# A gated delta-rule layer: two fp32 column sums on TensorE become pairs of rounded-and-rest matmuls, ScalarE and GpSimd queues are reordered, and the gates are computed another way

## Reference, cut to what matters

```
xn   = layernorm(x)
q, k, v = silu(conv4(xn @ Wq)), silu(conv4(xn @ Wk)), silu(conv4(xn @ Wv))
q, k = q / sqrt(sum(q*q) + 1e-6) * 128**-0.5,  k / sqrt(sum(k*k) + 1e-6)
g    = -exp(A_log) * softplus(xn @ Wf1 @ Wf2 + dt_bias)      # 8 decay groups a head
beta = sigmoid(xn @ Wb)
for t: S = S*exp(g);  delta = beta*(v - k.S);  S += k (x) delta;  o = q.S
y    = o * silu(xn @ Wg + bg)
y    = y * rsqrt(mean(y*y) + 1e-5) * norm_w
x1   = x + y @ Wo
out  = x1 + MoE(layernorm(x1))     # 2 of 6 experts per batch row
```

## Time and profile before

| | |
|---|---|
| median of 3 runs | 5799.16 us (5796.24 to 5802.64) |
| the profiled execution's own time | 5794.63 us |
| its span, first to last instruction | 5792.9 us |
| busy share of the span: PE, DVE, ACT, POOL | 96%, 77%, 52%, 30% |
| granted TensorE clock, mean | 0.987 of full speed |
| gates block | to 222.9 us |
| units | 222.9 to about 4976 us |
| mixture | from there to the end |

### The profile page before, as it was taken

One profiled execution on the slowest core, in us unless ns is written; L12 is line 12 of the kernel. 1 busy time (PEld: TensorE's weight loads), 2 busy tenths in 40 slices (PEclk: granted clock), 3 DMA queues, 4 the chain that ended last, 5 costly groups with the idle time before them and its releaser, 6 DMA issues. The chain is left out here.

```text
span 5792.9 us, 89715 instructions
## 1 busy us (share of the span) xinstructions
PE 5546.4 (96%) x30136; PEld 3878.3 (67%) x30136; DVE 4480.6 (77%) x9483; ACT 3000.7 (52%) x5573; POOL 1735.1 (30%) x1766
## 2 busy tenths in 40 slices
PE   5599999999999999999999999999999999899999
PEld 2377777777777777777777777777777777444444
DVE  7688888888888888888888888888888888211110
ACT  3456666665556566666666666555656665201110
POOL 2233333333333333333333333333333333000000
PEclk8799999999999999999999999999999999999999
DMA  2101110101111111111111111111111110231221
GB/s 76 46 28 37 30 37 28 36 27 36 30 37 30 37 30 36 31 30 37 30 37 30 36 29 35 28 37 30 37 30 38 30 30 24 99 111 51 78 76 49
DMA packets 183711, 235.84 MB, mean 41 GB/s; under 512 B 25048, under 2 KB 128088, under 8 KB 179168
## 3 DMA queue, kind: packets, MB, share of 16 engines
q1 hardware_dynamic: 111072, 188.22, 10.8%
q10 hardware_dynamic: 72192, 41.95, 2.4%
HBM read 183.75 MB, written 46.38 MB: 40 GB/s over the span
## 5 line engine op out<-in xcount | busy, mean ns | idle before, releaser
L685 PE MATMUL bank<-xT,weights 128*128 128x512 f32 x4096 | 2125.4, 606 | 33.5 <-PEq L155 33.5
L1339 POOL TENSOR_TENSOR KR<-KR,decay_u 128x256 f32<-128x256 f32 x768 | 632.2, 823 | 1544.3 <-PE bank L712 1534.5
L712 PEld LDWEIGHTS bank<-KQ,KR 128*128 128x128 f32 x7168 | 906.3, 191 | 191.5 <-issue 180.9
L712 PE MATMUL bank<-KQ,KR 128*128 128x128 f32 x7168 | 960.7, 276 | 7.0 <-DVE KQ L965 6.1
L950 DVE SCALAR_TENSOR_TENSOR conv<-pre,taps,conv 128x512 f32<-128x512 f32 x1152 | 935.8, 812 | 17.2 <-ACT conv L1167 8.0
L965 DVE TENSOR_TENSOR KQ<-KQ,decay_u 128x512 f32<-128x512 f32 x896 | 788.9, 880 | 143.9 <-PE bank L712 143.0
L987 DVE COPY_PREDICATED all_pairs<-level_mask,bank 128x256 f32<-128x256 int32 x1792 | 822.6, 523 | 0.0
L685 PEld LDWEIGHTS bank<-xT,weights 128*128 128x128 f32 x4096 | 662.8, 191 | 186.3 <-issue 164.0
L736 PEld LDWEIGHTS bank<-T_inv,pairs 128*128 128x128 f32 x1536 | 270.4, 189 | 535.8 <-ACT T_inv L1213 290.4
L736 PE MATMUL bank<-T_inv,pairs 128*128 128x128 f32 x1536 | 495.4, 407 | 82.5 <-ACT T_inv L1213 81.9
L1213 ACT ACTIVATE T_inv<-bank 128x256 fp32r<-128x256 f32 x640 | 247.2, 386 | 601.7 <-PE bank L754 597.6
(11 more groups left out here) (168 smaller groups left out, 9214.4 us busy)
## 6 DMA issues: line engine op xcount, KB each, us to landing
decay_u<-decay_scratch SPq DMA_DIRECT2D x128, 510.0 KB
beta_u<-beta_scratch SPq DMA_DIRECT2D x128, 256.0 KB
y_scratch<-y_rn ACTq DMA_DIRECT2D x128, 256.0 KB, 2.3
y_in<-y_scratch SPq DMA_DIRECT2D x32, 1024.0 KB, 4.8
xt<-in_L_attn_hidden_states SPq DMA_DIRECT2D x8, 1024.0 KB, 5.3
x_in<-in_L_attn_hidden_states SPq DMA_DIRECT2D x32, 256.0 KB, 5.1
out<-o_out ACTq DMA_DIRECT2D x32, 256.0 KB, 2.0
w<-in_L_ffn_W SPq DMA_DIRECT2D x8, 704.0 KB, 5.0
```

The source lines that it names most:

```text
L685: last = nc.tensor.matmul(bank[w % 2][:], weights[par][:, w, k, :], xT[:, k, u % J * UC:(u % J + 1) * UC], start=k == 0, stop=k == KC - 1)
L712: last = nc.tensor.matmul(to[:, :, i], KR[:, cols(i)], second if i < COUPLES else second[:, :, ::-1, ::-1], start=True, stop=True)
L1339: nc.gpsimd.tensor_tensor(firsts, firsts, second.to_broadcast([P, 2, UC >> (l + 2), 1 << l]), ALU.mult).then_inc(keys_scaled.sem, 1)
```

## The change

- `diagonal` no longer multiplies tiles. GpSimd forms the elementwise product of KR and q_hat (`diagonal_product`), ScalarE rounds it to fp32r (`round_diagonal`, now first in its step), GpSimd takes the exact rest (`diagonal_left`), and PE sums both over partitions with a tile of ones. It moves behind `level(2)`, as does `keep_diagonal` on DVE (before `scale(2)`).
- `y_sums` is done in the same way, with `y_squares_left` on GpSimd; the 1/128 moves into the logarithm.
- ScalarE's order: `take_t(4)` and `take_x(4)` come before `square_output` and `silu_gate`; the key square comes behind `take_t(5)`.
- GpSimd's order: `squares_left` of queries and keys moves from before levels 5 and 6 to behind levels 3 and 4; the one of y stands behind level 5.
- Gates: beta is computed as 64 rows of 128 (batch row by head) instead of 16 rows of 512, log(1+e) by a polynomial of degree 11 without a reciprocal, the two stores have a semaphore each, Wf1's product comes before beta's on PE, and ScalarE computes the next chunk's inverse deviation before it touches the decay logits.

```diff
+
+
+        LOG1P = [1.0, -0.4999997913837433, 0.33332496881484985, -0.24986496567726135,
+                 0.19885820150375366, -0.16087622940540314, 0.12377995997667313, -0.08188040554523468,
+                 0.04100657254457474, -0.013187825679779053, 0.001986696384847164]
+        SP_STEPS = len(LOG1P)
 
...
                 sp.wait_ge(beta_steps, j * 2 + 2)
-                sp.dma_start(beta_scratch[:, bass.ds(j, 1), :].rearrange("h a c -> h (a c)"),
-                             b_out[:]).then_inc(scratch_stored, 16)
...
-                dve.wait_ge(scratch_stored, j * 32 + 32)
+                dve.wait_ge(beta_stored, j * 16 + 16)
                 nc.vector.reciprocal(b_out[:], b_den[:]).then_inc(beta_steps, 1)
...
                 dve.wait_ge(z_exp_ready, j + 1)
-                chained(1, nc.vector.tensor_scalar(z_s[:], z_exp[:], 2.0, None, ALU.add))
-                chained(2, nc.vector.reciprocal(z_s[:], z_s[:]))
-                chained(3, nc.vector.tensor_tensor(z_s[:], z_s[:], z_exp[:], ALU.mult))
-                chained(4, nc.vector.tensor_tensor(z_s2[:], z_s[:], z_s[:], ALU.mult))
-                chained(5, nc.vector.tensor_scalar(z_sum[:], z_s2[:], ATANH[-1], None, ALU.mult))
-                for k, c in enumerate(ATANH[-2:0:-1]):
-                    chained(6 + k, nc.vector.scalar_tensor_tensor(z_sum[:], z_sum[:], c, z_s2[:], ALU.add, ALU.mult))
-                chained(SP_STEPS, nc.vector.scalar_tensor_tensor(z_sum[:], z_sum[:], ATANH[0], z_s[:], ALU.add, ALU.mult))
+                chained(1, nc.vector.tensor_scalar(z_sum[:], z_exp[:], LOG1P[-1], None, ALU.mult))
+                for k, c in enumerate(LOG1P[-2::-1]):
+                    chained(2 + k, nc.vector.scalar_tensor_tensor(z_sum[:], z_sum[:], c, z_exp[:], ALU.add, ALU.mult))
                 nc.vector.scalar_tensor_tensor(softplus[:], z[:], 0.0, z_sum[:], ALU.max,
                                                ALU.add).then_inc(softplus_ready, 1)
...
 
-            def chunk(j, first):
+            def chunk(j, first, last):
                 for k in range(KC):
...
+                act.wait_ge(f1_done, j + 1)
+                nc.scalar.activation(f1_sb[:], bank[4][:], ACT.Copy).then_inc(f1_ready, 1)
                 act.wait_ge(beta_logits_done, j + 1)
                 if not first:
                     act.wait_ge(beta_steps, j * 2 - 1)
-                nc.scalar.activation(b_exp[:], bank[5][0:H, :], ACT.Exp, scale=-1.0).then_inc(beta_exp_ready, 1)
-                act.wait_ge(f1_done, j + 1)
-                nc.scalar.activation(f1_sb[:], bank[4][:], ACT.Copy).then_inc(f1_ready, 1)
+                nc.scalar.activation(b_exp[:], bank[5][0:B * H, 0:P], ACT.Exp, scale=-1.0).then_inc(beta_exp_ready, 1)
                 if not first:
                     decays(j - 1)
+                if not last:
+                    inverse_std(j + 1)
...
-                        last = nc.tensor.matmul(bank[5][0:H, :], wb[:, k, :], xT[:, k, bass.ds(j * UC, UC)],
-                                                start=k == 0, stop=k == KC - 1)
-                    last.then_inc(beta_logits_done, 1)
-                    for k in range(KC):
                         last = nc.tensor.matmul(bank[4][:], wf1[:, k, :], xT[:, k, bass.ds(j * UC, UC)],
                                                 start=k == 0, stop=k == KC - 1)
                     last.then_inc(f1_done, 1)
+                    for k in range(KC):
+                        for b in range(B):
+                            last = nc.tensor.matmul(bank[5][0:B * H, 0:P], wb_each[:, k, b, :],
+                                                    xT[:, k, bass.ds(j * UC + b * P, P)],
+                                                    start=k == 0 and b == 0, stop=k == KC - 1 and b == B - 1)
+                    last.then_inc(beta_logits_done, 1)
                     pe.wait_ge(f1_ready, j + 1)
                     nc.tensor.matmul(bank[6][:], wf2[:], f1_sb[:], start=True, stop=True).then_inc(f2_done, 1)
...
         def load_unit(h, j, odd):
-            sp.dma_start(beta_u[:], beta_scratch[bass.ds(h, 1), bass.ds(j, 1), :].rearrange("a b c -> (a b) c")
-                         .to_broadcast([P, UC])).then_inc(unit_loaded.sem, 16)
+            sp.dma_start(by_batch(beta_u[:]), beta_scratch[j, :, h, :].unsqueeze(0).to_broadcast([P, B, P])) \
...
                     return
-                wait(pe, unit_ready, m, 1)
-                if b is not None:
-                    wait(pe, k_rows_ready, b, 1)
-                for i in range(B):
-                    last = nc.tensor.matmul(bank[4][:, cols(i)], KR[:, cols(i)], in_order(q_hat[:, cols(i)], i), start=True, stop=True)
-                last.then_inc(diag_done.sem, 1)
+                wait(pe, diag_rest_ready, m, 1)
+                wait(pe, pairs_ready, m, 2)
+                nc.tensor.matmul(bank[4][:], ones_r[:], diag_round[:], start=True, stop=False)
+                nc.tensor.matmul(bank[4][:], ones_r[:], diag_rest[:], start=False, stop=True).then_inc(diag_done.sem, 1)
...
-                    wait(pe, pairs_ready, m, l)
+                if l == 1 and b is not None:
+                    wait(pe, k_rows_ready, b, 1)
+                if l >= 2:
+                    wait(pe, pairs_ready, m, l - 1)
+                if l == 3:
+                    wait(pe, diag_kept, m, 1)
                 to = bank[3 + l % 2][:].rearrange("p (k b m s) -> p k b m s", k=2, b=B, s=1 << l)
...
                     wait(pe, sums_taken, a, 2)
-                wait(pe, y_sq_ready, c, 1)
-                nc.tensor.matmul(bank[2][:], mean_ones[:], y_sq[:], start=True, stop=True).then_inc(y_sums_done.sem, 1)
+                wait(pe, y_rest_ready, c, 1)
+                nc.tensor.matmul(bank[2][:], ones_r[:], y_sq[:], start=True, stop=False)
...
             inverse_z(1)
             project(2, (2,))
-            diagonal()
             level(0)
...
             level(2)
+            diagonal()
             inverse_xt(3)
             output()
...
-                if b is not None:
-                    wait_apart(dve, pairs_kept.sem, pairs_kept.at(b, 1), dve_waits_passed)
+                wait_apart(dve, pairs_ready.sem, pairs_ready.at(m, 2), dve_waits_passed)
                 nc.vector.copy_predicated(by_batch(all_pairs[:, 1]), on_each_batch(ident[:].bitcast(I32)),
-                                          by_batch(bank[4][:])).then_inc(pairs_ready.sem, 1)
+                                          by_batch(bank[4][:])).then_inc(diag_kept.sem, 1)
 
...
+                if l >= 1:
+                    wait_apart(dve, pairs_ready.sem, pairs_ready.at(m, l), dve_waits_passed)
+                elif b is not None:
+                    wait_apart(dve, pairs_kept.sem, pairs_kept.at(b, 1), dve_waits_passed)
+                if l == 2:
+                    wait_apart(dve, diag_kept.sem, diag_kept.at(m, 1), dve_waits_passed)
                 for turned in range(2):
...
             correct_delta(0)
             add_identity_to_z(1)
-            keep_diagonal()
...
             correct_delta(1)
             convolve(0, (2,))
+            keep_diagonal()
...
 
-            def silu_squares(w):
+            def silu_keys_queries(w):
                 if a is None:
                     return
                 wait(act, qk_conv_steps, a, (w + 1) * (TAPS - 1))
                 if w == 0 and m is not None:
-                    wait(act, diag_done, m, 1)
+                    wait(act, diag_product_ready, m, 1)
                     wait(act, unit_ready, m, 1)
                 nc.scalar.activation(silu[:, w], conv[:, w].rearrange("p b t -> p (b t)"),
                                      ACT.Silu).then_inc(silu_ready.sem, 1)
+
+            def square(w):
+                if a is None:
+                    return
                 wait(act, silu_ready, a, w + 1)
                 nc.scalar.activation(squares[:, w], silu[:, w], ACT.Square).then_inc(squares_ready.sem, 1)
+
+            def round_diagonal():
+                if m is None:
+                    return
+                wait(act, diag_product_ready, m, 1)
+                if b is not None:
+                    wait(act, diag_done, b, 1)
+                nc.scalar.activation(diag_round[:], diag_product[:], ACT.Copy).then_inc(diag_rounded.sem, 1)
 
             def silu_v():
...
                 wait(act, y_sums_done, c, 1)
-                nc.scalar.activation(y_rn[:], bank[2][:], ACT.Ln, bias=ln_eps[:, 0:1]).then_inc(y_sums_free, 1)
+                nc.scalar.activation(y_rn[:], bank[2][:], ACT.Ln, bias=ln_eps[:, 0:1], scale=1.0 / P).then_inc(y_sums_free, 1)
...
+            round_diagonal()
             silu_v()
             take_t(1)
             take_x(1)
@@ -1291,13 +1333,15 @@
             take_x(2)
             take_t(3)
             take_x(3)
-            silu_squares(0)
+            silu_keys_queries(0)
+            square(0)
+            take_t(4)
+            take_x(4)
             square_output()
             silu_gate()
```

(80 more changed lines are left out.)

37 lines of the change are left out of this document (23 added, 14 removed).

## The result

The changed kernel takes 5813.53 us (median of 9 runs, 5808.74 to 5833.07) against 5799.71 for the kernel before beside it (9 runs, 5796.24 to 5803.55): 1.0031 times as long, 95% interval 1.002 to 1.0041. The prediction said 5725.

A forecast was written before the change was run, and what follows sets the result against it. PE was taken to bound the units, DVE close behind: 5794.6 us less 60 for the gates and 13 for the units made 5721.6; with the median's 4.5 above it 5726, stated as 5725, range 5590 to 5785.

The forecast's parts named there:

- What bounds: Units bound by PE (98% busy) with DVE (89%) close behind; the gates block by something else.
- B: Step from the key taps' end through silu, square and `take_t(5)` to `inverse_z(6)`: 1.65 us, falling to 1.0.
- PE's savings: Diagonal and `y_sums` as fp32r pairs of 0.55 us save PE 0.34 + 0.31 = 0.65 us a step.
- A: Step from level 0's start to the last key tap's end on DVE: 18.16 us, rising to 19.91 through GpSimd collisions.
- C: Rest of the step, from `inverse_z(6)` to the next level 0, PE's stream: 16.90 us, falling to 15.70.
- The gates: Gates block before the units: period 23.3 us falling to 15.2, 60 us saved, between 45 and 66.
- Rival 2: Slower units: GpSimd wins every race; product also holds off a tap and first `scale`, step 37.6, 5854 us; chance 0.10.

The follow-up runs named there:

- no_y_late_keys: `no_y` with GpSimd's square and rest of the keys moved from behind level 4 to behind level 5: 5807.6 us, 1.0009 of the kernel before.
- y_new_old_squares: Changed kernel with GpSimd's query and key squares back before levels 5 and 6, y's pair behind level 3: 5810.09 us, 1.0015 of before.
- fill: Changed kernel plus two fp32 matmuls of zeros per step in PE's wait before `inverse_z(6)`: 5797.38 us, 0.9992 of the kernel before.
- fill_y_new: `y_new_old_squares` plus the same two matmuls of zeros per step in PE's wait: 5744.45 us, 0.9903 of the kernel before.
- no_y: Changed kernel with the sum of y squared in fp32 as before, query and key squares behind levels 3 and 4: 5839.31 us, 1.0066 of before.
- split_y: Changed kernel, query and key squares back before levels 5 and 6, y's product behind level 3, its rest behind level 6: 5619.41 us, 0.9686 of before.
- gates_only: Kernel before plus only the gates part (beta by rows, polynomial logarithm, two semaphores, beta's loads in four pieces): 5746.06 us, 0.991 of before.
- act_order: `gates_only` plus ScalarE's new order alone; diagonal, y sums and GpSimd's order as before: 5670.14 us, 0.9775 of the kernel before.
- no_y_old_squares: Changed kernel with y's sum in fp32 as before and GpSimd's query and key squares before levels 5 and 6: 5643.67 us, 0.9731 of before.

## Why the prediction was wrong

**What bounds.** Right. Stretch B and the 0.17 us that PE waits once the taps are free show the loop named: taps, silu, `take_t(5)`, `inverse_z(6)`.

**PE's savings.** Right: pairs of 0.55 us, and 0.30 of the usual step for y.

**A.** Right: from 2509.19 to the taps' end at 2529.15, 19.96 us (predicted 19.91). The diagonal's rest at L1092 (1.18), the first tap freed (0.80), the wait for the diagonal (0.54; predicted 0.4), `scale(2)` at 0.68 and the two taps at 2.71 all stand as written.

**B.** Right: 2530.13 - 2529.15 = 0.98 us (predicted 1.0).

**C, the step that failed.** Predicted 15.70, measured 37.28 - 19.96 - 0.98 = 16.34. C was taken as PE's stream alone, the C of before less what PE saves. The walk followed POOL's queries' pair into A, but placed the keys' pair, which the change moves to behind level 4, nowhere, and did not ask whether DVE's chain behind the taps (state, halo copy, `scale(4)`, pairs, identity) still comes in time for `inverse_xt(5)`. A usual step of the changed kernel:

```profile
2567.29 0.96 DVE L961 COPY pre<-pre 128x24 f32<-128x24 f32 x1
2568.17 0.68 DVE L989 TENSOR_TENSOR KQ<-KQ,decay_u 128x512 f32<-128x512 f32 x1
```

```profile
2567.18 1.04 POOL L1391 TENSOR_TENSOR conv<-silu 128x512 f32<-128x512 f32 x1 [1.39 <-ACT silu L1205]
```

```profile
2568.96 1.10 PE L735 MATMUL bank<-KQ,KR 128*128 128x128 f32 x8
2570.29 0.44 PE L782 MATMUL bank<-X,ZI 128*128 128x128 f32 x2 [0.23 <-DVE ZI L1043]
```

The keys' product starts after the silu, and the halo copy behind it ends at 2568.25, 0.03 after the product. `inverse_xt(5)` stands 1.33 us behind its level in place of 0.81. (In the 16 steps without the copy it is `scale(4)` that meets the product, with 1.44 as shown above, and 1.26 in place of 0.81.) Before had nearly the same collision, with the queries' product:

```profile
2573.97 0.79 DVE L937 COPY pre<-pre 128x24 f32<-128x24 f32 x1
```

but there DVE's identity was done about 0.36 us before PE asked for it. With B 0.65 us shorter PE asks earlier, and the copy is 0.17 longer: together that turns the slack into a delay of about 0.5. `no_y_late_keys` takes the pair away and gets 0.55, and `y_new_old_squares`, in which no pair meets the halo copy either, has a C of 36.73 - 19.96 - 0.99 = 15.78, just the 16.98 - 0.89 - 0.31 of the sum. The other 0.08 is that I measured C of before on the mean step, 36.71, while that of a usual step is 36.79.

**The clock, which had no term.** I treated a wait of PE as worth its length. In the changed kernel 19 steps are 1.07 us longer (20.4 us in the profiled execution). `fill` gets 16 us back and `fill_y_new` 66 by adding work to PE. Shown is that filling the wait ends the falls, twice. The falls are not scattered: 12 of the 18 distances between them are 150.2 us (four steps), and in `y_new_old_squares` 36 of 40 are 75.1 us (two steps). This suggests that it hangs on where a wait lies in time; that is not shown, and why `no_y` with the same wait has only 4 long steps is open.

**The gates.** 53.2 us where I took 60. The period is 17.1 us, not 15.2. PE, one period, from transposes to transposes:

```profile
118.99 2.87 PE L443 MATMUL bank<-ident,xt 128*128 128x128 f32 x16 [2.47 <-DVE xt L322]
123.81 5.12 PE L448 MATMUL bank<-xT,wf 128*128 x8 [1.95 <-ACT xT L382]
128.86 3.71 PE L453 MATMUL bank<-xT,wb_each 128*64 x32
...
136.09 2.91 PE L443 MATMUL bank<-ident,xt 128*128 128x128 f32 x16 [2.46 <-DVE xt L322]
```

and the window of that product's first half:

```profile
123.81:126.40 2.59, 2.59 (x3) 1.17 (x4) 2.45 (x5) 0.00 (x0) 0.00 (x0) 0.50 1.00 301
```

The first product, with 3.70 us in the earlier trace rows where it stood second, now stands first behind a wait and takes 5.12, half of it at clock 0.50. I had feared the lower clock for the second product and taken 4 us off for it; it is the first one that meets it. From the start of the transposes to the start of the second product it is 9.87 us instead of 8.07, which is nearly all of the period's miss. Six periods of 6.2 us saved, 37.2 instead of 48, and the last chunk's 15.2 instead of 17 are 12.6 us less; 5 of them I had taken off beforehand (4 for the clock, 1 for beta's weights), and the rest, less 0.8 gained elsewhere in the block, makes the 7 us. DVE's own chain came out as written: the reciprocal of beta 0.94 us, ten multiply-adds 7.23.

```profile
119.19 0.94 DVE L333 RECIPROCAL b_out<-b_den 64x128 f32<-64x128 f32 x1
...
120.45 7.23 DVE L345 SCALAR_TENSOR_TENSOR z_sum<-z_sum,z_exp 128x512 f32<-128x512 f32 x10
```

**The rivals.** Rival 2 (slower) is what came, with 0.10; its threshold of 0.57 us a step more than before was right: the mean step is 0.62 longer. Its reason was half right: one more lost race (the halo copy, or `scale(4)`), not one of the two it named, and in place of the second one the clock. The forecast left 0.10 us of gain in a step, so a single lock of half a microsecond, whose kind I had just read three times from the rows, decided the sign of the units; 0.10 was too low for that.

**In sum.** Against the profiled executions the miss is 5827.0 - 5721.6 = 105.4 us: the keys' pair 70 (0.55 x 127), the clock 20.4, the gates 7, the base step 10 (0.08 x 127), and smaller terms of both signs that come to -2. The median of the changed kernel lies 13.5 us below its profiled execution, and the 5725 stands 3.4 above the sum of 5721.6, so that the medians show 88.5 of it.

## What to carry to other kernels

Give moved work its position on both sides: for every GpSimd instruction that a change adds or moves, write down which DVE instruction it will run beside, and what waits for that one; here the same 2.3 us of GpSimd work cost from nothing (`no_y` against the changed kernel) to 1.2 us a step. When a reordering changes a loop that is nearly in balance, measure the parts apart: ScalarE's order alone gave 76 us, and was hidden in a kernel that came out slower. A wait of TensorE of over a microsecond can cost more than its length; look at the granted clock just behind it.

## What the runs showed of the hardware

- A DVE instruction on 512 columns with two SBUF inputs that was behind running GpSimd work ended 0.54 to 0.56 us after it (all 786 cases in the changed kernel, all 593 in `split_y`). With two such DVE instructions in a row, a GpSimd instruction could come in between (the taps' 2.71 us, with `scale_keys(4)` between them). A small copy with one SBUF input waited too: the halo copy ended 0.03 to 0.04 us after the running GpSimd instruction and took 0.96 us in place of 0.17 (`no_y_late_keys`).
- PE's clock was at its lower level for most of the 3.5 us after waits of 1.35 us, in 4 (`no_y`), 19 or 41 of 127 steps of versions whose wait is equally long, mostly at even distances; with waits of 0.17 to 0.39 us (`gates_only`, `act_order`, `no_y_old_squares`, `split_y`) the units had at most one long step. Filling the wait with 1.45 us of matmuls on zeros brought the long steps to none.
- The lower clock cost 1.07 us a step in the changed kernel and 1.64 in the two versions where the usual step was shorter.
